# One transformer block on one core: query lengths moved into the exponential, keys scaled tile by tile, a padded stream, and finer steps in a new order

## What is computed

```python
def _layer(x, wqkv, qs, ksc, wo, lg, lb, w1, b1, w2, b2):
    h = shift_token(x)                  # upper half of the columns comes from the row before
    q, k, v = jnp.split(h @ wqkv, 3, axis=-1)       # 8 heads of 64
    q = l2norm(q) * qs
    k = l2norm(k) * ksc
    q, k = rotary_xpos(q, k)
    o = local_attention(q, k, v)        # windows of 64 see themselves and the one before
    x = x + o @ wo
    h = shift_token(x)
    h = (h - mu) / jnp.sqrt(var + 1e-05) * lg + lb
    a, g = jnp.split(h @ w1 + b1, 2, axis=-1)
    h = a * jax.nn.gelu(g, approximate=False)
    return x + h @ w2 + b2
```

## Time and profile before

| | before |
|---|---|
| median of 3 runs | 967.3 us |
| lowest and highest | 965.48 and 968.2 us |
| the profiled execution, its own time | 966.96 us |
| its span, first to last instruction | 965.0 us |
| PE, weight loads | 786.4 us busy (81%), 556.3 us (58%) |
| DVE | 668.0 us busy (69%) |
| ACT | 659.3 us busy (68%) |
| POOL | 539.6 us busy (56%) |
| PE clock granted, mean | 0.942 of full |

### The profile page before, as it was taken

How to read it: one execution, slowest core, us unless ns; L and a number is a source line. 1 busy time by engine, 2 the same in 40 slices (tenths; PEclk the granted TensorE clock), 3 DMA queues, 4 the chain that set the end, 5 groups by cost and what they waited for, 6 DMA issues and landing times.

```text
span 965.0 us, 19306 instructions
## 1 busy us (share of the span) xinstructions
PE 786.4 (81%) x7151; PEld 556.3 (58%) x7151; DVE 668.0 (69%) x1588; ACT 659.3 (68%) x1545; POOL 539.6 (56%) x324
## 2 busy tenths in 40 slices
PE   4456788879889989888969979888888989888874
PEld 4334566656556666655657656656565666656543
DVE  4566876685687877586887967486787776676732
ACT  0234766867576985877786886877675887868672
POOL 2046853493956653394985643293966690576600
PEclk9668789999899999999999999999999999999997
DMA  6000000000000000000000000000000000000000
GB/s 206 0 12 1 12 2 1 1 1 2 1 2 1 23 2 22 2 1 1 1 1 2 23 1 23 1 2 1 1 1 2 12 2 13 2 1 2 1 1 22
DMA packets 12275, 9.85 MB, mean 10 GB/s; under 512 B 1040, under 2 KB 11288, under 8 KB 12184
## 3 DMA queue, kind: packets, MB, share of 16 engines
q1 hardware_dynamic: 12184, 8.64, 3.0%
HBM read 6.54 MB, written 2.10 MB: 9 GB/s over the span
## 4 chain that ended last, share of the span: by engine, by line
PE 40%; DVE 20%; ACT 19%; issue 11%; POOL 9%; DMA 0%; SPq 0%; POOLq 0%; ACTq 0%; DVEq 0%
ACT probs L964 7%; PE pair L696 6%; PE mixed L727 5%; POOL qk L1494 4%; PE dense L831 4%; PE pair L759 3%; DVE space L1393 3%; DVE q_norm L1398 3%; PE dense L795 3%; PE dense L796 2%; PE dense L797 2%; DVE qk L1195 2%; PE dense L908 2%; ACT squares L1083 2%; ACT probs_t L972 2%
## 5 line engine op out<-in xcount | busy, mean ns | idle before, releaser
L1494 POOL TENSOR_TENSOR qk<-space 128x512 f32<-128x512 f32 x128 | 186.4, 1463 | 58.0 <-DVE q_norm L1398 55.1
L1454 POOL TENSOR_TENSOR root<-power,minus_half 128x32 f32<-128x32 f32 x32 | 174.0, 5438 | 4.6 <-DVE power L1404 4.6
L964 ACT ACTIVATE probs<-pair,neg_max 128x128 f32<-128x128 f32 x512 | 138.3, 402 | 18.9 <-DVE neg_max L1215 18.5
L1393 DVE TENSOR_TENSOR space<-dense,tables 128x512 f32<-128x512 f32 x128 | 87.5, 684 | 36.9 <-ACT space L1087 35.2
L908 PE MATMUL dense<-wq_hi,h_hi 128*128 128x512 f32 x192 | 90.2, 470 | 26.6 <-DVE space L1393 10.9
L1491 POOL TENSOR_TENSOR space<-space,tables 128x512 f32<-128x512 f32 x64 | 82.7, 1293 | 50.7 <-ACT space L1087 50.7
L696 PE MATMUL pair<-eye_s,probs 128*128 128x128 f32 x512 | 80.9, 292 | 34.9 <-ACT probs L964 34.7
L1215 DVE TENSOR_REDUCE neg_max<-pair 128x4 f32<-128x512 f32 x128 | 82.0, 684 | 35.2 <-PE pair L759 35.1
L1083 ACT ACTIVATE squares<-dense 128x512 f32<-128x512 f32 x128 | 79.1, 618 | 39.5 <-PE dense L910 38.6
L696 PEld LDWEIGHTS pair<-eye_s,probs 128*128 128x128 f32 x512 | 59.1, 146 | 56.2 <-ACT probs L964 51.9
L1398 DVE TENSOR_REDUCE q_norm<-squares 128x8 f32<-128x512 f32 x128 | 86.4, 675 | 0.0
(11 more groups left out here) (166 smaller groups left out, 1809.2 us busy)
## 6 DMA issues: line engine op xcount, KB each, us to landing
x_in<-n_L_attn_embeddings_dram SPq DMA_DIRECT2D x8, 256.0 KB, 3.0
out_dram<-hn SPq DMA_DIRECT2D x8, 256.0 KB, 2.4
qk<-in_L_ffn_wqkv_dram SPq DMA_DIRECT2D x1, 1536.0 KB, 6.2
qk<-in_L_ffn_w_dram SPq DMA_DIRECT2D x1, 682.0 KB, 7.5
wo_s<-in_L_ffn_wo_dram SPq DMA_DIRECT2D x2, 256.0 KB
o_t<-in_L_wmod_dram SPq DMA_DIRECT2D x1, 384.0 KB, 3.3
probs<-const_rotary_dram SPq DMA_DIRECT2D x1, 256.0 KB, 3.6
band_s<-const_band_dram SPq DMA_DIRECT2D x1, 256.0 KB, 7.8
```

The lines of the kernel that those rows point to most:

```text
L964: last = act.activation(probs[:, ring, hh, :], banks[m][:, hh * P:(hh + 1) * P], ACT.Exp, bias=neg_max[:, ring, hh:hh + 1], scale=1.0)
L1393: dve.tensor_tensor(turned_s[:, t % 2, m, :].rearrange("p (h a b) -> p h a b", h=HEADS, a=2), halves[:, :, ::-1, :], rot(layer, t, 2 * m + 1),
L1454: return pool.tensor_tensor(to, of, minus_half[:, 0:of.shape[-1]], ALU.pow)
L1494: pool.tensor_tensor(qk[s][:, t, m * INNER:(m + 1) * INNER], turned_c[:, t % 2, m, :], turned_s[:, t % 2, m, :], ALU.add).then_inc(added, 1)
```

## The change

- **Query lengths.** The queries are no longer multiplied by their inverse lengths. The scores of a query row are scaled inside the exponential instead: ACT's exponential gets the inverse length as its scale operand (from SBUF, one number per row), and DVE multiplies the negative maximum by it, one more instruction on 4 columns for each of the 128 halves of a tile.
- **Keys per tile.** The keys are multiplied by their inverse lengths tile by tile (512 columns, 64 times) where queries and keys of two tiles were multiplied together (2048 columns, 32 times). PE may transpose a tile's queries before any root is there.
- **The root.** POOL's one `pow` on 32 columns becomes a seed of two DVE instructions and ten small POOL instructions (three Newton steps), each waiting for the one before. The `pow` on 4 columns for the normalisations stays.
- **Padded stream.** `y_new` and `y_t` get a zero column ahead of each sequence, so that the shift by a row is a view. ACT's copies into `shifted` go (64 instructions); DVE rounds the two halves of the columns with one instruction each; of `h_lo` POOL takes the lower half, DVE the upper. For `ff.stats` PE transposes in 8 pieces of 64 columns where it had 4 of 128.
- **Folded norm weights.** `ln_g` and `ln_b` go into `w1` and `b1` once at the start (12 matmuls with one column on PE, some DVE work). ACT copies `ff.norm`'s bank straight to `h_hi`; DVE takes `h_lo` from the same bank. DVE's `h_hi` and POOL's `h_lo` of the feed-forward go.
- **Values across windows** are copied by 64 DMAs from SP's queue where ACT did it.
- **The start.** The weights come layer by layer; ACT rounds `wq`, DVE takes the rests.
- **The order.** Turns, flips, mixes and exponentials are steps by halves of a tile, POOL's cosine product and additions, DVE's table products and sums are steps of their own, `up` is two steps per chunk, and `ORDER` is written anew.

```diff
@@ PE, attention @@
                 if what == "turn":
-                    pe.wait_ge(qk_ready, 2 * before + t // 2 + 1)
+                    m = step[3]
+                    if m == 0:
+                        pe.wait_ge(added, 2 * tau + 1)
+                    else:
+                        pe.wait_ge(keys_ready, tau + 1)
@@ PE, ff.stats @@
-                    done(turn_four(to, lambda k: flat(shifted)[:, k * P:(k + 1) * P]),
-                         i, slot, step)
+                    for k in range(TILES):
+                        at = (k % 2) * P
+                        for part in range(2):
+                            last = pe.matmul(to[:, k * P + part * WIN:k * P + (part + 1) * WIN],
+                                             y_t[stream(slot)][:, k // 2, at + 1 - part:at + 1 - part + P],
+                                             eye_s[:, part * WIN:(part + 1) * WIN], start=True, stop=True)
@@ ACT @@
 -                            last = act.activation(probs[:, ring, hh, :], banks[m][:, hh * P:(hh + 1) * P], ACT.Exp,
-                                                  bias=neg_max[:, ring, hh:hh + 1], scale=1.0)
+                        last = act.activation(probs[:, ring, hh, :], banks[m][:, hh * P:(hh + 1) * P], ACT.Exp,
+                                              bias=neg_max[:, ring, hh:hh + 1],
+                                              scale=query_root(s, t, m)[:, hh:hh + 1])
...
-            def shift(src, done_sem):
-                act.activation(shifted[0:P // 2, :, :], src[0:P // 2, :, :], ACT.Copy)
-                act.activation(shifted[P // 2:P, :, 1:SEQ], src[P // 2:P, :, 0:SEQ - 1], ACT.Copy).then_inc(done_sem, 1)
...
-                    act.activation(hn[:, :], src[:, :], ACT.Identity, scale=columns[:, ROW_LN_G + layer:ROW_LN_G + layer + 1],
-                                   bias=columns[:, ROW_LN_B + layer:ROW_LN_B + layer + 1]).then_inc(empty(i, slot, step), 1)
+                    act.activation(h_hi[:, :], bank(i, slot, step)[:, :], ACT.Copy).then_inc(ff_hi, 1)
...
-                        act.activation(v_cross[s][half_rows, t // 2, :, 0:DH], heads[half_rows], ACT.Copy)
@@ DVE @@
-                dve.tensor_tensor(rows, rows, root[:, :].rearrange("p (h o) -> p h o", o=1)
-                                  .broadcast_to([P, 4 * HEADS, DH]), ALU.mult).then_inc(qk_ready, 1)
+                    dve.wait_ge(added, 2 * (4 * before + t) + 2)
+                    dve.wait_ge(qk_rooted, 2 * before + t // 2 + 1)
+                    keys = qk[s][:, t, INNER:].rearrange("p (h d) -> p h d", d=DH)
+                    dve.tensor_tensor(keys, keys, key_root(s, t).rearrange("p (h o) -> p h o", o=1)
+                                      .broadcast_to([P, HEADS, DH]), ALU.mult).then_inc(keys_ready, 1)
...
+                    dve.wait_ge(max_self, 2 * tau + m + 1)
+                    dve.wait_ge(qk_rooted, 2 * before + t // 2 + 1)
+                    dve.tensor_tensor(neg_max[:, ring, :], neg_max[:, ring, :], query_root(s, t, m),
+                                      ALU.mult).then_inc(maxed, 1)
...
-                    dve.tensor_scalar(power[:, :], q_norm[:, :], 1e-24, None, ALU.max).then_inc(qk_powered, 1)
+                    dve.tensor_scalar(half[:, :], q_norm[:, :], 1e-24, 0.5, ALU.max, ALU.mult).then_inc(seed_self, 1)
+                    dve.wait_ge(seed_self, pair_ + 1)
+                    dve.tensor_scalar(root[s][p][:, 0, :].bitcast(I32), half[:, :].bitcast(I32), -0.5, RSQRT_SEED, ALU.mult,
+                                      ALU.add).then_inc(qk_seeded, 1)
@@ POOL @@
-                inverse_root(root[:, :], power[:, :]).then_inc(qk_rooted, 1)
+                y, z = to[:, 0, :], to[:, 1, :]
+                pool.tensor_tensor(z, y, half[:, :], ALU.mult).then_inc(qk_newton, 1)
...
+                for k in range(3):
+                    pool.tensor_tensor(scratch[:, :], y, z, ALU.mult).then_inc(qk_newton, 1)
+                    pool.wait_ge(qk_newton, count + 1)
+                    pool.tensor_tensor(scratch[:, :], threes[:, :], scratch[:, :], ALU.subtract).then_inc(qk_newton, 1)
+                    pool.wait_ge(qk_newton, count + 2)
+                    if k < 2:
+                        pool.tensor_tensor(to[:, :, :], to[:, :, :], scratch[:, :].rearrange("p (o h) -> p o h", o=1)
+                                           .broadcast_to([P, 2, 32]), ALU.mult).then_inc(qk_newton, 1)
...
+                    else:
+                        pool.tensor_tensor(y, y, scratch[:, :], ALU.mult).then_inc(qk_rooted, 1)
@@ SP @@
+                    for t, half_ in ((2 * p, 1), (2 * p + 1, 0)):
+                        sp.wait_ge(*read_at(i, slot, (PROJ, "tile", t, 2)))
+                        rows = slice(WIN * half_, WIN * half_ + WIN)
+                        sp.dma_start(v_cross[s][rows, p, :, :], v[s][rows, t, :, :]).then_inc(v_crossed[s][p], 16)
@@ ORDER, ACT, turn 1, slot 1 (cut) @@
-        1:a.turn.1 1:a.score.0 1:a.score.1 1:a.flip.0 1:ff.norm 1:a.flip.1 1:a.out.0 1:ff.up.0 1:ff.up.1
+        1:a.turn.2.1 1:ff.up.0 1:a.turn.3.0 1:a.turn.3.1 1:a.score.2.0 1:a.score.2.1 1:ff.up.1 1:a.flip.2.0
```

1164 lines of the change are left out of this document (682 added, 482 removed).

## The result

| | before | after |
|---|---|---|
| median of 4 runs | 967.75 us | 1075.76 us |
| lowest and highest | 965.48, 968.42 us | 1073.33, 1078.2 us |
| ratio, 95% interval | | 1.1121, 1.1081 to 1.116 |
| span of the profiled run | 965.0 us | 1076.4 us |
| clock granted to PE, mean | 0.942 | 0.92 |

A forecast was written before the change was run, and what follows sets the result against it. It took no engine as full, with PE nearest and its waits, ACT between its steps, as what can change. 54 us saved less 50 added gave 963; the order, up to 939, made it 948, range 930 to 963 (outer 910 to 988).

The forecast's parts named there:

- Operand and loads: On ACT: the exponentials' scale operand adds 24 us (0 to 31), the 30 more table loads add 15 us.
- The savings less the small additions: Whole chain: 54 us saved, less 7 for scaling the maximum and 4 for second seed instruction, transposes and such.
- The order: New order of steps, played through: 963 down to 939 us; 948 taken, two fifths of the way up.
- the contention: POOL's small root instructions, stretched by DVE's keys' products beside them: would lose up to 10 of the root's 17 us.
- The start: Kernel start: DVE's rests of weights come earlier in the new order, saving 2 us.
- the conversion from busy time to span: All engines: busy time times share on the chain, 28% for ACT, 29% for DVE, 47% for the exponentials.
- the copies: ACT's 64 shifts and 64 copies to `v_cross` go: 22 us at 28%, taken as 15 less 3 for DVE's rounding.
- the terms of the root and the keys: POOL's root saves 17 us (4 at the dear end); DVE's keys-only product, 0.6 us per tile, saves 14 us.
- PE's share: PE's eight transposes where there were four, booked with the second seed instruction and such: 4 us added.
- the sign on which the order rests: Attention pace in slots 2 and 3: the forecast fails if it isn't under 53 us.
- the second rival: Hidden: the root and keys' 31 us come to little, DVE is late next, the order gives nothing: 965 us; chance 0.10.
- The third: ACT paces the attention: its extra 89 us fall between PE's scores and flips, four fifths counting: 980 us; chance 0.22.

The follow-up runs named there:

- order run: The changed kernel's instructions with the step tables put back to the order of the kernel before: 998.2 us, ratio to the kernel before 1.034.
- gelus together: The changed kernel in its own order, but the three gelus of each feed-forward stand together on ScalarE: 1076.5 us; with Identity for the gelu 1057.1 us.
- whole tiles: The changed kernel in the order of before, without scale operand or scaled maximum, queries and keys of a tile multiplied together: 963.9 us, ratio to before 0.996.
- the run with the scale column: The kernel before with a column of ones from SBUF as the exponential's scale instead of the constant 1.0: 1004.9 us, ratio 1.0368.

## Why the prediction was wrong

The 108 us, from the runs: the order 77.6 (the loads 49.0, the placing 28.6), the operand 35.1 in the old order, everything else -4.6. The sum is 108.1. Against the forecast three steps failed with about equal weight. Operand and loads were booked at 39 us and cost 84. The savings less the small additions were booked at 43 us and gave 5. The order was booked as a gain of 15 us and cost 29. The three misses are 45, 38 and 44 us, together 127 of the 128 us between 948 and 1075.8.

**Right, mechanism and size.** The exponentials' busy time (190 for 190), their share of the chain (10% for "9% or more"), 70 table loads, ACT's total (675.8 for 670), POOL's share of the chain (2% for under 5%). The operand takes 0.09 to 0.10 us per instruction, as bounded: 44 us of ACT in three pairs of runs. The five groups of the root's small instructions on POOL sum to 85.8 us for 90; with 22.5 us of idle time between them a root takes 3.4 us where I had 2.9. One of the five:

```profile
L1691 POOL TENSOR_TENSOR scratch<-root 128x32 f32<-128x32 f32 x96 | 24.5, 255 | 7.5
```

So the contention that I had drawn from the Trainium skill ("GPSIMD Engine Reference", section 8), up to 10 of the 17 us, does not show in these small instructions: the groups have 0.25 us at 32 columns and 0.32 at 64, and the fastest and the median one of L1691 are alike (0.250 and 0.252 us). My 0.20 and 0.27 were too short from the start. It does show on DVE's side, under step 2. POOL's additions came down from 1.46 to 1.34 us, 16 us of POOL. The start gained more than booked (the first output projection begins at 127.75, have 147.64; the order run has 143.82, so most of it is the new order's), but the later slots took it back. What `h_lo` on DVE, the folded norm and the shifts on ACT are worth was not tried singly.

**Wrong step 1, the conversion from busy time to span.** I took each edit's busy time times the share of its engine or group on the chain, 28% or 47%. For ACT alone the runs give this:

| edit on ACT | change of its busy time | change of the time | ratio |
|---|---|---|---|
| loads between exponentials, in before | +42.6 | +48.2 | 1.13 |
| operand, new order | 44.4 | 47.4 | 1.07 |
| operand, in before | +43.9 | +37.3 | 0.85 |
| operand, old order | 43.4 | 35.1 | 0.81 |
| all gelu tables, new order | 93.1 | 55.6 | 0.60 |
| all gelu tables, gelus together | 43.6 | 19.4 | 0.44 |
| `v_cross` copies, in before | 31.7 | 8.6 | 0.27 |
| `v_cross` copies, whole tiles | 30.0 | 5.8 | 0.19 |
| all gelu tables, old order | 47.4 | 6.6 (11 by ratios) | 0.14 (0.22) |

One engine, prices from 0.14 to 1.13. What stands between PE's scores and its flips counts nearly in full or more; what stands where ACT waits for PE counts for a fifth. The 24 us of the operand should have been 35 to 47, the 15 us of the loads some 40 to 50. Of the copies only those to `v_cross` were tried: 11 us by my share, 6 to 9 measured. My own sentence that the copies "block nobody but ACT itself" was right and should have set the lower price; that the loads "stand between the exponentials of an attention" should have set the higher one.

**Wrong step 2, the terms of the root and the keys.** The pieces of "issue" and `pow` on the chain, 36 us, are not what goes when the `pow` goes: 3 us in the kernel before, 6 in whole tiles, for 17 predicted. The run with the scale column fits: with ACT a little later, GpSimd's share of the chain fell from 9% to 1% by itself. The keys' product I took as a quarter of 2.53 us, 0.6. It takes 1.08 us in the mean, 67.0 us in all for 38. The quarter was not far off, though; the mean hides two kinds. POOL and DVE in the after trace, and a free product last:

```profile
267.45 1.27 POOL L1738 TENSOR_TENSOR qk<-space 128x512 f32<-128x512 f32 x1
267.60 1.67 DVE L1631 TENSOR_TENSOR qk<-qk,root 128x512 f32<-128x512 f32 x1 [0.58 <-POOL root L1701]
268.68 1.73 POOL L1729 TENSOR_TENSOR space<-space,tables 128x512 f32<-128x512 f32 x1
269.79 1.17 DVE L1631 TENSOR_TENSOR qk<-qk,root 128x512 f32<-128x512 f32 x1
...
389.10 0.69 DVE L1631 TENSOR_TENSOR qk<-qk,root 128x512 f32<-128x512 f32 x1 [0.68 <-POOL root L1701]
```

POOL's addition ends at 268.72 and DVE's product, begun beside it, at 269.27; POOL's next ends at 270.41 and the second product at 270.96, again 0.55 us later. Of the 64 products 35 take 0.68 to 0.73 us. The other 29 begin while POOL is at an instruction of 510 or 512 columns, and each ends 0.55 us behind that one; they take up to 1.78 us. These holds are 25 of the 29 us that the group has over my 38. In the order run they are 13 us. The fastest products of 1024 and 2048 columns take 1.21 and 2.28 us. So the length was nearly right, and what I left out is POOL's work of 1.3 us in front of it, which the new order puts there more often; PE waits 15.5 us for these keys, and in the order run none of that wait is listed. The run without the operand in the old order gives the net of all these terms, 4.6 us, where I had 54 - 11 = 43.

**Wrong step 3, PE's share.** I had put the eight transposes among "4 us" with the second seed instruction. They take 22 us more of PE than the four transposes, 15 more than four products, and with four products the time was 10.6 us less.

**Wrong step 4, the order.** It is the largest part of the loss, but not the whole of its sign: in the old order the changed instructions are already 31 us slower than the kernel before. I had it worth 28 us, or 15 after caution; it costs 28.6 without the gelu's loads and 77.6 with them. I had played slot 1 at 56 us and slot 2 at 47. They take 58 and 62 in the turn shown above. The hand counted engine time and the first waits within the block, but not what the block had covered where it stood before: PE's waits for the exponentials in the second half of each attention. Moving it alone costs 129.5 us, with 36 us of new waits for `h_lo` that the changed kernel does not have. The hand also kept the old length of PE's products, though PE was granted less of its clock: in slots 1 and 2 the windows have 0.86 to 0.94, where those of the kernel before have 0.92 to 1.00. And it took no account of DVE's key products being held by POOL. I had named a pace of 53 us in slots 2 and 3 as the sign on which the order rests; it was 58 and 64.

**Two slips in the sums.** 28 us off 963 are 935, not 939, so two fifths of the way up from there would have been 946. And in the second rival the 31 us of root and keys were not put back: without them the sum is 963 + 31 = 994, not 965. Its mechanism, savings that come to little while other waits end just behind, is the one that the runs show for the root, and I had given it 0.10 and a range that ended at 970.

**The rivals.** The third had the mechanism: exponentials and loads between PE's scores and flips. It was to decide where 89 us times the share passes the rest, at two thirds; the shares were 0.8 to 1.1 for the operand and for loads between exponentials, and 0.6 for all 68 loads of the new order. At 980 us it was still far too low, since it kept 54 us of savings of which 5 net exist and 15 us for the order that were a loss. Its chance of 0.22 rested on the argument that PE has feed-forward products at those places. The trace shows that it has not enough: 1.82 us idle at 422.26.

**The table load's own price.** From the Trainium skill ("ScalarE: Activation LUTs", "What ACT_TABLE_LOAD costs") I had set 2.66 us with a drain beside 1.28 without. At 472.70 the load starts 0.02 us behind the end of the squares, 1.28 us long: no drain shows here either. That the kernel loses 1.6 us per load (48.2 / 30) comes from what waits behind it.

**Open.** How the 28.6 us of the placing divide between the projections' block, the keys held by POOL, the start of the feed-forward and PE's clock.

## What to carry to other kernels

Before an edit's busy time is turned into time, look at who waits at its own place: here, on the engine that stands between two steps of the busiest one, a microsecond cost 0.8 to 1.1, and elsewhere on the same engine about a fifth. A chain's share says where the last wait was, not what is saved without it; adding a small delay elsewhere in the unchanged kernel shows at once whether the wait is real. When a block of work is moved, price what it covered at the place that it leaves. And where a mean duration is scaled to another size, look at the fastest and the slowest first: they may be two kinds.

## What the runs showed of the hardware

- A product with the identity by which four blocks of 128 x 128 (fp32) are turned leaves 128 records and 17.9 us over 16 feed-forwards, the same four as transposes 64 records and 10.7 us. Eight products with 64 columns take 33.0 us, eight with 128 columns 33.5.
- A DVE product of a 512-column SBUF tile by a column per head, begun while POOL is at a tensor-by-tensor instruction of 510 or 512 columns, ends 0.55 us behind POOL's (29 of 64 in the changed kernel, 0.84 to 1.78 us); alone it takes 0.68 to 0.73 us. With 1024 columns the lag is 1.08 us, with 2048 it is 2.15. Beside POOL's `pow` on 4 columns three of them were not held.
- A column as the scale operand of an exponential of 128 columns from PSUM costs 0.09 to 0.10 us each (138.3 to 184.5 us for 512), even when it holds only ones.
- Two table loads and a one-element activation between them take 2.79 us in a row with no gap over 0.02 us.
- PE's products of 512 columns follow each other every 0.43 us right behind a wait of 3.30 us and every 0.23 us some 3 us later, the two levels of its clock, 1.2 and 2.4 GHz; behind a wait of 0.84 us they kept 0.23 us. So PE's busy time is no fixed cost: 786.4 us in the kernel before, 802.1 with the loads between its exponentials, with the same instructions.
